# Other key tiles for four kinds of side work, and GpSimd in place of ScalarE for splitting the queries

## The reference, cut to what matters

```
xn = layernorm(x)                                  # first norm, per token
q, k, v = xn @ Wq + bq, ctx @ Wk + bk, ctx @ Wv + bv   # 32 wide: 8 heads of 4; ctx has 1601 rows
o = softmax(q k^T * scale) v                       # per head, over all 1601 keys
x = x + tanh(g_xattn) * (o @ Wo + bo)              # output projection
y = layernorm(x)                                   # second norm
scores = softmax(y @ router_w + router_b)          # 8 experts
# each expert takes its 512 best tokens; up 256->1024, relu, down, times score, added back
out = x + tanh(g_ffn) * scatter_add(experts)
```

## Time and profile before

| what | value |
|---|---|
| median of 3 runs | 595.37 us (594.85 to 595.54) |
| the profiled execution, its own time | 594.75 us |
| span of the profile | 592.9 us |
| PE, DVE, ACT, POOL busy | 551.4, 444.1, 397.4, 196.8 us |
| granted TensorE clock, mean | 0.995 of full speed |

### The profile page before, as it was taken

How to read it: one execution, slowest core, us unless ns; L and a number is a source line. 1 busy time by engine, 2 the same in 40 slices (tenths; PEclk the granted TensorE clock), 3 DMA queues, 4 the chain that set the end, 5 groups by cost and what they waited for, 6 DMA issues and landing times.

```text
span 592.9 us, 12821 instructions
## 1 busy us (share of the span) xinstructions
PE 551.4 (93%) x5043; PEld 318.6 (54%) x5043; DVE 444.1 (75%) x811; ACT 397.4 (67%) x774; POOL 196.8 (33%) x193
## 2 busy tenths in 40 slices
PE   6798899998999989999999998899999999999994
PEld 4433333333333333333333344469889898898974
DVE  3889879996798967989897258746767868677541
ACT  2587789987888878898888830044665646655651
POOL 3058030024420063400158010240735626346234
PEclk9999999999999999999999999999999999999998
DMA  8600000000000000000000004122735556356133
GB/s 280 241 2 1 1 1 3 2 1 38 2 36 2 2 37 1 37 2 1 37 38 2 36 19 140 34 60 72 163 112 117 144 136 148 108 107 163 16 36 35
DMA packets 23807, 35.80 MB, mean 60 GB/s; under 512 B 3459, under 2 KB 16196, under 8 KB 23620
## 3 DMA queue, kind: packets, MB, share of 16 engines
q1 hardware_dynamic: 17604, 26.59, 13.8%
q0 software_dynamic: 6144, 8.39, 8.3%
HBM read 26.59 MB, written 8.39 MB: 59 GB/s over the span
## 4 chain that ended last, share of the span: by engine, by line
PE 67%; DVE 18%; ACT 5%; issue 4%; POOL 3%; DMA 1%; POOLq 0%; ACTq 0%; DVEq 0%; SPq 0%
PE ps L1719 15%; PE ps L1726 15%; PE ps L1488 12%; DVE mquart L1016 11%; PE ps L1475 6%; PE ps L1454 6%; PE ps L1384 2%; ACT probs L741 2%; PE ps L1345 2%; POOL xn L528 2%; PE ps L1360 1%; PE ps L1697 1%; PE ps L1672 1%; ACT osb L641 1%; PE ps L1513 1%
## 5 line engine op out<-in xcount | busy, mean ns | idle before, releaser
L1016 DVE TENSOR_REDUCE mquart<-ps 128x2 f32<-128x802 f32 x256 | 241.9, 988 | 33.4 <-PE ps L1454 30.2
L741 ACT ACTIVATE probs<-ps 128x512 f32<-128x512 f32 (+1 forms) x416 | 222.9, 599 | 24.0 <-PE ps L1475 20.8
L1488 PE MATMUL ps<-probs,vp 128*32 128x256 f32 (+1 forms) x1664 | 132.7, 391 | 4.5 <-ACT osb L641 4.5
L1454 PE MATMUL ps<-kpad,qrows 64*128 64x401 bf16 x512 | 90.6, 337 | 3.7 <-DVE mquart L1016 3.1
L1475 PE MATMUL ps<-qfull,kpad 64*128 64x256 bf16 (+1 forms) x832 | 89.8, 272 | 2.8 <-ACT x L762 0.9
L1313 DVE TENSOR_TENSOR h1l<-hf,h1h 128x512 fp32r<-128x512 f32 x64 | 44.4, 693 | 56.0 <-ACT hf L868 56.0
L867 ACT ACTIVATE h1h<-ps,b1T 128x512 fp32r<-128x512 f32 x64 | 44.0, 687 | 53.8 <-PE ps L1719 53.6
L1726 PE MATMUL ps<-w2h,h1h 128*128 128x256 f32 x256 | 73.8, 288 | 2.2 <-DVE h1l L1313 1.5
L1726 PE MATMUL ps<-w2l,h1h 128*128 128x256 f32 x256 | 72.4, 283 | 0.0
L1726 PE MATMUL ps<-w2h,h1l 128*128 128x256 f32 x256 | 72.3, 283 | 0.0
L1475 PEld LDWEIGHTS ps<-qfull,kpad 64*128 64x128 bf16 (+1 forms) x832 | 38.9, 96 | 48.2 <-ACT probs L741 25.1
(11 more groups left out here) (198 smaller groups left out, 682.3 us busy)
## 6 DMA issues: line engine op xcount, KB each, us to landing
w1raw<-in_L_ffn_w SPq DMA_DIRECT2D x16, 512.0 KB, 4.6
w2raw<-in_L_ffn_w SPq DMA_DIRECT2D x16, 512.0 KB, 4.7
xs<-in_x SPq DMA_DIRECT2D x4, 512.0 KB, 7.7
ctx_sb<-in_ctx SPq DMA_DIRECT2D x3, 512.0 KB, 5.8
out<-xs SPq DMA_DIRECT2D x3, 512.0 KB, 2.6
x_rows<-x SPq DMA_DIRECT2D x3, 512.0 KB, 2.6
b2b<-in_L_ffn_b SPq DMA_DIRECT2D x1, 1024.0 KB, 11.1
out<-xs SPq DMA_DIRECT2D x2, 256.0 KB, 2.0
```

The costliest lines, as they stand in the source:

```text
L741: nc.scalar.activation(out_p, ps[0:w, next_bank(), :], ACT.Exp, scale=float(SCALE)).then_inc(s_ex, 1)
L1016: nc.vector.tensor_reduce(mquart[:, u % 2, t, a, :, kq], ps[:, b:b + 2, 0:MAXW], AX.X, ALU.max).then_inc(s_mr, 1)
L1454: last = mm(ps[:, bank + b, 0:MAXW], qrows[band(b), g, q:q + P], kpad[band(b), g, a, lo:lo + MAXW], start=True, stop=True)
L1488: last = mm(ps[32 * hh:32 * hh + 32, PV, 0:UW], vp[0:w, kt, g, hh, :], probs[0:w, step % PROBS, hh, :], start=(kt == 0), stop=(kt == NKT - 1))
```

## The change

Four edits, all in the attention stage.

1. `LN1_AT` is now a table from (u, kt) to (chunk, token tile): chunk 2's statistics stand at (1, 9) to (1, 12), chunk 3's at (5, 9) to (5, 12), each `ln1_aggr` at kt 0 of the unit after.
2. The output projection moves from (0, 10) to (0, 12), the second norm's statistics from (1, 2)-(1, 5) to (1, 4)-(1, 7).
3. The second turn of x2 moves from (2, 8) to (2, 7), the router from (2, 10) to (2, 9).
4. For the queries of chunks 1 to 3 (six blocks, n >= 10) ACT writes xf only; POOL writes c1 from xf, then t1, c2 and the rows, all four in a row in `split_queries`. ACT's wait on `s_t1` is one block looser for them, since c1 is no longer ACT's there.

```diff
-        O_THIS, O_LAST, BACK_AT, WO_AT = (2, 4), (0, 4), (0, 7), (0, 10)
+        O_THIS, O_LAST, BACK_AT, WO_AT = (2, 4), (0, 4), (0, 7), (0, 12)
-        X2_AT, ROUTER_AT = ((2, 6), (2, 8)), ((2, 10), (2, 12))
+        X2_AT, ROUTER_AT = ((2, 6), (2, 7)), ((2, 9), (2, 12))
-        LN1_AT, LN2_AT = ((0, 0), (0, 1), (0, 2), (0, 3)), ((1, 2), (1, 3), (1, 4), (1, 5))
+        LN1_AT = {(u, NKT - CT + t): (c, t) for c, u in ((2, 1), (3, PER_CHUNK + 1)) for t in range(CT)}
+        LN2_AT = ((1, 4), (1, 5), (1, 6), (1, 7))
@@ gpsimd
+            def split_queries(c, g, n):
+                pool.wait_ge(s_t1, n)
+                pool.wait_ge(s_xf, n + 1)
+                nc.gpsimd.tensor_scalar(c1[:, :], xf[:, g, :], cst[:, C_MASK:C_MASK + 1], None, ALU.mult).then_inc(s_c1, 1)
+                split_rest(pool, nc.gpsimd, n, g, CW)
+                pool.wait_ge(s_t1, n + 1)
+                nc.gpsimd.tensor_scalar(c2[:, :], t1[:, :], cst[:, C_MASK + 1:C_MASK + 2], None, ALU.mult).then_inc(s_c2, 1)
+                split_rows(pool, nc.gpsimd, n, CW, qrows[:, g, CW * c:CW * c + CW])
...
                     for g in range(NG):
-                        split_rest(pool, nc.gpsimd, n + g, g, CW)
-                        split_rows(pool, nc.gpsimd, n + g, CW, qrows[:, g, CW * (c + 1):CW * (c + 2)])
+                        split_queries(c + 1, g, n + g)
@@ scalar, qk_bias
-                at_least(act, s_t1, n)
+                at_least(act, s_t1, n if n < len(BLOCKS) else n - 1)
...
-                nc.scalar.activation(c1[:, 0:w], ps[:, bank, 0:w], ACT.Identity, ...).then_inc(s_c1, 1)
+                if n < len(BLOCKS):
+                    nc.scalar.activation(c1[:, 0:w], ps[:, bank, 0:w], ACT.Identity, ...).then_inc(s_c1, 1)
                 nc.scalar.activation(xf[:, half, 0:w], ps[:, bank, 0:w], ACT.Identity, bias=bias).then_inc(s_xf, 1)
@@ scalar, loop over units
-                    if c + 1 < NC and (r, kt - 2) in Q_AT:
-                        split_middle(NKB + NG * (c + 1) + Q_AT.index((r, kt - 2)), "q", CW)
@@ vector, loop over units
-                    if 0 < c < LAST and (r, kt) in LN1_AT:
-                        ln1_stats(c + 1, LN1_AT.index((r, kt)))
-                    if 0 < c < LAST and (r, kt - 1) == LN1_AT[-1]:
-                        ln1_aggr(c + 1)
+                    if (u, kt) in LN1_AT:
+                        ln1_stats(*LN1_AT[u, kt])
+                    if kt == 0 and (u - 1, NKT - 1) in LN1_AT:
+                        ln1_aggr(LN1_AT[u - 1, NKT - 1][0])
```

More of the change, by code:

```diff
@@ L651, in qk_bias @@
                 mask = C_MASK + 2 * (kind == "k")
-                nc.scalar.activation(c1[:, 0:w], ps[:, bank, 0:w], ACT.Identity, bias=biasneg[:, col:col + 1],
-                                     scale=cst[:, mask:mask + 1]).then_inc(s_c1, 1)
+                if n < len(BLOCKS):
+                    nc.scalar.activation(c1[:, 0:w], ps[:, bank, 0:w], ACT.Identity, bias=biasneg[:, col:col + 1],
+                                         scale=cst[:, mask:mask + 1]).then_inc(s_c1, 1)
                 nc.scalar.activation(xf[:, half, 0:w], ps[:, bank, 0:w], ACT.Identity, bias=bias).then_inc(s_xf, 1)
```

## The result

The changed kernel takes 592.26 us (median of 5 runs, 591.86 to 592.66) against 595.46 us (5 runs, 594.85 to 595.84) beside it: ratio 0.9947, 95% interval 0.9932 to 0.9961. 3.2 us are gained where 5.9 were forecast. The profiled execution took 591.86 us, span 590.1.

What follows compares the result with a forecast made beforehand. PE, DVE and ACT run in step, DVE nearest its limit, fed by PE. Terms -4.8 - 3.3 + (1.3 + 1.5 + 0.3) - 0.9 + 0 = -5.9 us: 588.85 from 594.75, 589.4 for the median; range 585.5 to 593.3.

Steps and rivals of the forecast that it cites:

- first blocks of edit 4, three times: Units 1, 5, 9: without c1 on ACT the second query projection starts 0.7 us sooner, in three chunks.
- the rest of units 1-2, 5-7, 9-11: Second query blocks -0.4 us each, arriving statistics +1.3, +1.5 and +0.3, moved output projection -0.3 a chunk.
- DVE eats it: Rival: no DVE slack in units 1, 5, 9, second block's and output projection's gains lost; -2.4, 593.0 us; chance 0.20.
- Edit 1, what goes: Units 4 and 8: xn ready early, each becomes unit 12 plus xn's transposes, 17.2 us; -4.8 us together.
- Edit 4, ACT: Query blocks: without c1, xf frees the bank sooner; -0.7 us first block, -0.4 second, three chunks, -3.3.
- The ACT rival: ACT limits after each query projection, so all it gives up returns: -8.2 there, 584.6 us in all; chance 0.11.
- Edit 1, what comes: Ends of units 1 and 5: 1.64 us of DVE statistics a chunk; +1.3 in unit 1, +1.5 in unit 5 with edit 2.
- Edit 4, POOL: POOL's query blocks take 5.1 us each; x2 ready at +12.4, turned at about +18 after the second projection; no cost.
- s: Time of POOL's new one-operation tensor_scalar on 128x512, taken as 1.2 us, range 0.6 to 2.4.
- The slower rival: POOL late: with s above about 2.6 us PE waits for x2 in units 6 and 10; 600.9 us at s = 4; chance 0.06.
- Edits 2 and 3: Output projection -0.3 us a chunk; later second-norm statistics put +0.62 on DVE in the open, +0.3 in unit 9; edit 3 zero.
- Unit 13 only shifts: Moving unit 13's second-norm statistics costs nothing: x2 ready at about 311 instead of 309, turned at 318.

Runs made afterwards that it cites:

- e_gate: Changed kernel; POOL also waits for the last mparts of the attention (unit 14) before the third of four pairs of weight blocks; 588.93 us, ratio 0.9892.
- e_c1_act: Changed kernel with that POOL wait and first-norm statistics of chunks 2, 3 under the query projections, c1 of the six blocks back on ACT; 588.64 us, one run.
- e_split: Kernel before with edit 4 alone (POOL forms c1 and c2 of six query blocks), all places old; 591.51 us, ratio 0.9929.
- e_places: Kernel before with edits 2 and 3 alone (new key tiles for output projection, second-norm statistics, second x2 turn, router); 598.89 us, ratio 1.0054.
- e_norm1: Kernel before with edit 1 alone (first-norm statistics of chunks 2 and 3 at the ends of units 1 and 5); 591.51 us, ratio 0.993.
- e_gaps: Changed kernel; each of POOL's 16 weight instructions waits for the one before, w1l now ahead of w2h; 589.34 us, one run.

## Why the prediction was right in direction and half short in size

Attention, from the `qfull` of unit 0 to the last `osb`, went from 280.77 to 277.89 us, -2.9. By the prediction's steps:

| step | forecast | found |
|---|---|---|
| units 4 and 8, first norm gone | -4.8 | -4.82 |
| first blocks of edit 4, three times | -2.1 | -2.0 |
| the rest of units 1-2, 5-7, 9-11 | +1.3 | +0.5 |
| unit 13 | -0.3 | -0.15 |
| unit 14, wait for `mparts` | 0 | +2.66 |
| unit 15, half clock behind that wait | 0 | +0.96 |

(The third row of the forecast is -1.2 + 3.1 - 0.6; found is the units' sum, -0.16 - 0.13 - 1.23, less the second row. Unit 14 and 15 are taken against *e_gate*.)

Without the last two rows the attention stage gains 6.5 us, and *e_gate*, which removes them, takes 588.93 us where 589.4 was forecast. That the changed kernel's 592.26 lies near the 593.0 of the rival *DVE eats it* is luck: that rival needs +4.5 us in the third row, and 0.5 was found there.

- *Edit 1, what goes*: right; unit 12 as a twin of unit 4 gave the size to 0.02 us.
- *Edit 4, ACT*: right between the projections (DVE's idle time under the second fell from 1.33 to 0.70, forecast 0.6), and c1 was its cause, as *e_c1_act* shows. Behind the second projection it is worth 1.26 - 0.67 = 0.59 net by *e_split*, where 0.4 was forecast. The ACT rival (-8.2) is out: *e_split* gives -3.8.
- *Edit 1, what comes*: the cost of the statistics depends on what else is there. Alone they cost 0.4 a chunk, with edit 4 1.11 in units 1 and 2 (forecast 1.3). With edit 4 the gain of the second block and the room for the statistics are the same DVE time: units 1 and 2 changed by +0.39 with edit 1, by -1.27 with edit 4, and by -0.16 with both, 0.7 short of the sum; in units 5 to 7 it is 1.0.
- *Edit 4, POOL*: s was 1.57, forecast 1.2, within its bounds, and far above the cast's 0.61. `x2` was ready 13.4 us after the second projection's end (forecast 12.4) and turned at 17.9 (18). The slower rival's mechanism did not occur at this place.
- *Edits 2 and 3*: for unit 9 the forecast puts the output projection at -0.3 and the second norm's statistics at +0.3; *e_places* has +0.01 there and 0.00 in unit 5, which fits the sum and can't tell the two apart. Unit 13 brought 0.14, not 0.3. Edit 3, put at nothing, brought 0.25 a chunk, within its bounds.
- *The step that failed* is the sentence "Unit 13 only shifts", with "`x2` is ready at about 311 instead of 309 and is turned at 318". The delay was followed to the next reader of `x2` and no further. Behind `ln2_apply` stand POOL's 16 weight instructions, 14.3 us in one row without a pause. The row ended 0.8 us after `mparts` began in the kernel before. What the rest of the change gains doesn't shift the two against each other (unit 14 keeps its 17.45 in *e_norm1* and *e_split*); edit 2 does, by the two key tiles, and they now overlap by 3.6 us. The delay itself was under-sized as well: counted from unit 12's `qfull`, `x2` was ready at +20.7 and is now at +24.2 (306.19 less 281.98), 3.5 us later and not 2. Two experiments remove the overlap (row sooner, row held back), a third puts pauses into the row, and each takes unit 14 to 17.8 or 18.0.

The Trainium skill (GPSIMD Engine Reference, 8 Key points) says that GpSimd shares its SBUF interfaces with VectorE and that DVE instructions with two SBUF inputs, or in a two-port mode, contend with it. This case agrees: `mparts` has two inputs in SBUF, while maxima (from PSUM) and statistics (one SBUF input) kept their 0.98 and 0.41 us beside a busy POOL. The casts that are held in *e_gaps* have one input; whether they run in a two-port mode no view shows. The prediction weighed a rule about GpSimd's speed and passed this one by.

## What to carry to other kernels

When a step is moved, follow the delay down its queue to the last instruction behind it, and ask of each which instruction of another engine it will now overlap. A long unbroken row of GpSimd work beside a DVE instruction with two SBUF inputs on the critical path is worth one semaphore wait that puts it behind, or pauses inside it. Put DVE's side work where DVE idles anyway (under a long matmul), and don't add the gains of two edits that draw on the same idle time.

## What the runs showed of the hardware that was not expected

The hold itself: 8 columns of subtraction at 0.20 us took 3.67 and 3.70 us in two kernels, to within 0.1 us of the end of POOL's row. It shows on a small scale in `mparts` of units 1, 5 and 9 of the changed kernel too: 0.56, 0.41 and 0.41 us, over when POOL's two-input L389 ends. Not every POOL instruction holds it to its end: in the kernel before, `mparts` took 0.20 us at 134.21, beside an L528 that ran from 134.15 to 135.40, and 0.43 us at 305.45, beside an L538 that ran to 306.51. Why, stays open. Maxima and statistics in the same stretch keep their times. Timelines of POOL and of DVE, unit 5 of the changed kernel:

```profile
155.08 1.17 POOL L389 TENSOR_TENSOR t<-xf,c 128x512 f32<-128x512 f32 x1
```
```profile
155.88 0.41 DVE L1041 TENSOR_TENSOR mparts<-nmax,mparts 128x8 bf16<-128x8 f32 x1
...
157.35 0.41 DVE L933 BATCH_NORM_STATS2 stats<-xs 128x6 f32<-128x256 f32 x1
157.69 0.97 DVE L1025 TENSOR_REDUCE mquart<-ps 128x2 f32<-128x802 f32 x1
```

And the clock. After PE's 2.60 us of idleness in the profiled execution of the changed kernel its granted clock is half. Windows from 321 to 326 us (length, then busy time of PE, PEld, DVE, ACT, POOL, then the clock):

```profile
321.00:322.00 1.00, 1.00 (x13) 0.32 (x15) 0.00 (x0) 0.97 (x3) 0.00 (x0) 0.85 0.00 0
322.00:323.00 1.00, 1.00 (x10) 0.38 (x12) 0.00 (x0) 0.89 (x2) 0.00 (x0) 0.50 0.00 0
...
324.00:325.00 1.00, 1.00 (x13) 0.31 (x12) 0.00 (x0) 0.58 (x2) 0.25 (x1) 0.50 0.00 0
325.00:326.00 1.00, 1.00 (x20) 0.28 (x12) 0.00 (x0) 0.92 (x3) 0.00 (x0) 0.94 0.00 0
```

It fell over a microsecond after PE had resumed (320.60), stayed at 1.2 GHz for some 3.4 us, and is what sets unit 15 of this execution (21.06 us) apart from its 20.10 in *e_gate*. In the profiled execution of *e_places*, after an idle time of 2.63 us at the same place, the clock stayed full (1.00 over 326 to 336 us) and unit 15 took 20.05. Its four other executions took 0.5 to 2.6 us longer, with a mean clock of 0.990 to 0.994 where the profiled one had 0.997. Of the changed kernel one execution had 0.997 too, and took 591.97 us, no less than the profiled one (591.86 at 0.992); so the mean clock alone doesn't give the time of a run, and the price of the fall is known from unit 15 of one trace alone. Whether the fall comes is not settled by the length of the idle time alone; what decides it stays open.
